# Two transpose banks, ACT as the queue for the weight and restack loads, and scratch stores issued back to back in an eight-core transformer layer

## The chip, the cores and the metric

The kernel runs on the 8 cores of one Trainium2 chip. Each core takes 4 of the 32 sequences, and the cores exchange nothing. The metric is the device time in microseconds (us) of the slowest core; lower is better. PE is TensorE, DVE is VectorE, ACT is ScalarE, POOL is GpSimd, and SP is SyncE, which only issues DMAs here. SPq in a row is the issue of a DMA by SP.

## The reference

One layer on x of shape (32, 2048, 1024): multi-query attention with 8 heads of 128, then a feed-forward part with 128 small experts (32 experts x 4 sets) whose tokens are picked inside groups of 32.

```
x = layernorm(x + attention(x))
# feed-forward, g = 32 tokens per group, s = 4 sets, e = 32 experts
logits   = einsum('bntd,des->bntes', grouped, Wc) + bc + tie
perm     = (logits == max over the tokens t of the group)
permuted = einsum('bntd,bntes->bnesd', grouped, perm)
inner    = relu(einsum('bnesd,esdf->bnesf', permuted, W1) + b1)
result   = einsum('bnesf,esdf->bnesd', inner, W2) + b2
x = layernorm(x + einsum('bnesd,bntes->bntd', result, perm))
```

## The kernel before

Every engine has one list of instructions, written out in program order: `inc(engine, semaphore, n, ...)` appends an instruction that counts a semaphore up when done, `wait(engine, mark)` appends a wait, and `gset`/`gwait` keep the mark after which a buffer may be used again. An engine does its list strictly in order, so a wait on it holds back all that stands behind.

A core does its 4 sequences (s = 0 to 3) one after the other:

1. Projections and attention, with layer norm 1 at the end (`ln1`, 16 ACT instructions, L243).
2. Logits. For each of 4 blocks of 512 tokens, ACT casts x2 to bf16 (`xtile_bf`, L558, 4 instructions); PE transposes it in 8 steps of 4 transposes into the one PSUM tile `pp_tr` (L567); DVE copies each step to `x2t` (L572); then 8 matmuls make the logits (L580), one more adds the tie term (L583), and DVE adds the bias (L588). `xtile_bf` has one buffer, given back by the last copy.
3. The selection: DVE makes `pmT` (L593, L598), and PE and DVE turn it in 16 steps through `pp_tr` into `pmt` (L605, L608).
4. Gather and first expert product, for each of 4 column quarters q4: ACT casts x2 to `x2b` (L627), PE gathers (L638), DVE and ACT evict to `gq` (L649), and PE multiplies by `w_1` (L669). `w_1` has two buffers.
5. Second expert product, restack, and scatter. `emit_e2(q4)` fills `rpn` by 64 casts, half on DVE and half on ACT (L734), with the quarter's weights `w_2t`. `emit_restack(q4)` moves `rpn` to `rpe` in another layout through the DRAM scratch `rp_scratch`: two halves of 64 partitions, each a 2 MB store (L752, 64 rows of 32 KB) and a 2 MB load (L757, pieces of 512 B). `emit_scatter(q4)` multiplies `rpe` by `pmT` (L770, L777) and adds to x2 on DVE (L784). The order of emission is e2(0), restack(0), e2(1), scatter(0), restack(1), e2(2), scatter(1), restack(2), e2(3), scatter(2), restack(3), scatter(3).
6. Layer norm 2 and the stores of y.

What sets the order around the restack: the casts of e2(q4+1) wait until restack(q4) is over (key `rpn`). A restack waits on SP for the scatter before it (key `rpe`) and for all 64 casts by 64 single waits. All four of its DMAs are in SP's list, with a wait on SP between each store and its load.

In sequence 0 the expert weights come as f32 through POOL (cast on the way) and are stored as bf16 to `cw1` and `cw2` by SP; later sequences load those copies from SP's list, `w_2t` for the next quarter at the end of each `emit_e2` (4 DMAs of 512 KB), and `w_1` for the next quarter at the start of a gather stage.

Of the kernel before, what the change touches and what calls it, by code (L numbers as in the profile page):

```python
# [26 lines left out]
def build_nc(cfg):  # L27
# [36 lines left out]
    def bump(n):  # L64
# [50 lines left out]
          for i in range(2)]  # L115
# [23 lines left out]
    pp_tr = nc.alloc_psum_tensor("pp_tr", [128, 512], BF16).ap()  # L139
    pp_w = nc.alloc_psum_tensor("pp_w", [128, 1024], F32).ap()  # L140
# [3 lines left out]
                "sWA", "sWB", "sWC", "sWD", "sWE", "sWS", "sS1a", "sS1b", "sS2", "sS3"]  # L144
# [125 lines left out]
    for s in range(NSEQ):  # L270
# [87 lines left out]
        for qb in range(NQB):  # L358
# [66 lines left out]
            def emit_epilogue_tensor(h):  # L425
                wait("tensor", epi["nm"])
                gwait("tensor", ("tr",))
# [9 lines left out]
                gset(("tr",), av)  # L437
# [66 lines left out]
        def w1_load(q4):  # L504
# [9 lines left out]
            return inc("sync", w1sems[1][q4 % 2], 16,  # L514
                       lambda e, q=q4: e.dma_start(out=w_1[q % 2], in_=cw1[q]))
        if s == 1:
            wait("sync", st_all_ws)
            wait("sync", st_s2_all)
            wait("sync", st_s1a); wait("sync", st_s1b)
        if s > 0:  # L520
            wait("sync", ln1)
        gw1 = {0: w1_load(0)}
        def w2t_load(q4, part):
# [16 lines left out]
            inc("sync", sem, 16, lambda e, q4=q4, c0=c0: e.dma_start(  # L540
                out=w_2t[0][:, c0: c0 + 2048], in_=cw2[q4][:, c0: c0 + 2048]))
            return inc("sync", sem, 16, lambda e, q4=q4, c0=c0: e.dma_start(
# [10 lines left out]
        for tb in range(NQB):  # L553
            cm = None
            gwait("scalar", ("xtbf",))
# [5 lines left out]
            wait("tensor", cm)  # L561
            gwait("tensor", ("x2t",))
            for c in range(CH):
                gwait("tensor", ("tr",))
                tvv = None
                for t4 in range(4):
                    tvv = inc("tensor", "sPE", 1, lambda e, c=c, t4=t4: e.transpose(  # L567
                        pp_tr[:, t4 * 128: t4 * 128 + 128],
                        xtile_bf[:, t4 * 1024 + c * 128: t4 * 1024 + c * 128 + 128],
                        c_ident))  # L570
                wait("vector", tvv)
                cv = inc("vector", "sDVE", 1, lambda e, c=c: e.tensor_copy(  # L572
                    x2t_stage[:, c * 512: c * 512 + 512], pp_tr[:, :]))
                gset(("tr",), cv)
            gset(("xtbf",), cv)
            wait("tensor", cv)
            gwait("tensor", ("pw", 0))
            lgv = None
            for c in range(CH):
                lgv = inc("tensor", "sPE", 1, lambda e, c=c: e.matmul(  # L580
# [22 lines left out]
        for tt in range(NT):  # L603
            gwait("tensor", ("tr",))
            tv2 = inc("tensor", "sPE", 1, lambda e, tt=tt: e.transpose(  # L605
                pp_tr[:, 0:128], pmT[:, tt * 128: tt * 128 + 128], c_ident))
# [339 lines left out]
```

How the kernel before makes its waits and increments, by code:

```python
    def inc(eng, sem, n, buildfn):  # L155
        cnt[sem] += n; v = cnt[sem]
        emit(eng, lambda e, b=buildfn, s=sem, n=n: b(e).then_inc(sems[s], n))
        return (sem, v)
# [1 line left out]
    def wait(eng, mark):  # L160
        if mark is None: return
        sem, v = mark
        emit(eng, lambda e, s=sem, v=v: e.wait_ge(sems[s], v))
```

## Time and profile before

| | before |
|---|---|
| median of 3 runs | 5153.95 us (5148.46 to 5167.36) |
| profiled execution, device time | 5157.47 us |
| its span on the slowest core (core 7) | 5155.9 us |
| spans of the 8 cores | 5117.7 to 5155.9 us |
| mean granted PE clock, by core | 0.654 to 0.663 of full speed |
| busy share PE / DVE / ACT / POOL | 51% / 29% / 35% / 0% |
| DMA traffic of the core | 324.85 MB, mean 63 GB/s |

No engine is busy for more than about half of the span. The chain of work that ended last tells better than the shares what the time consists of, and the timeline of one stage tells what each step there waits for.

### The profile page before, as it was taken

The numbers are of one execution on the slowest core, as the hardware profiler recorded it, in microseconds if no ns is written. First come the engines' busy times: TensorE is split into PE (matmuls) and PEld (weight loads), VectorE is DVE, ScalarE is ACT, GpSimd is POOL, SyncE is SP. The second block draws the span as 40 slices with busy tenths as digits, with TensorE's granted clock in tenths as the row PEclk, the third lists the DMA queues.
The fourth block names the chain that finished last, engine by engine and source line by source line (L and its number), as shares of the span: only waits on it lengthen the run. The fifth ranks groups of instructions, "written<-read, shape, count | busy, mean of one in ns | idle before, by whom it ended". The sixth has DMA issues, their size and how long they took to land.

```text
span 5155.9 us, 64669 instructions; the slowest of 8 cores (5117.7 to 5155.9 us)
## 1 busy us (share of the span) xinstructions
PE 2644.5 (51%) x19792; PEld 1414.7 (27%) x19792; DVE 1489.5 (29%) x3689; ACT 1824.3 (35%) x3808; POOL 18.2 (0%) x35
## 2 busy tenths in 40 slices
PE   4666636332566663543256665453317666546240
PEld 2333314211233331421123332242103333224110
DVE  2322135222232213432322211443223221144232
ACT  0455533210335563330134556232121455523113
POOL 0000000000000000000000000000000000000000
PEclk9687856555667885655576887555557688756555
DMA  4200042475310001036520000105651000100644
GB/s 84 58 17 17 9 98 67 99 152 114 98 41 17 17 6 53 34 82 148 113 95 17 17 17 16 43 34 118 127 122 70 17 17 17 55 20 18 147 98 130
DMA packets 174811, 324.85 MB, mean 63 GB/s; under 512 B 5654, under 2 KB 136982, under 8 KB 168986
## 3 DMA queue, kind: packets, MB, share of 16 engines
q1 hardware_dynamic: 166554, 281.39, 21.3%
q0 software_dynamic: 7936, 39.33, 4.4%
q8 instruction: 184, 3.01, 0.2%
q14 instruction: 137, 1.12, 0.1%
HBM read 239.95 MB, written 120.07 MB: 70 GB/s over the span
## 4 chain that ended last, share of the span: by engine, by line
PE 43%; ACT 18%; DMA 16%; issue 11%; DVE 10%; SPq 1%; ACTq 0%; DVEq 0%; POOL 0%; POOLq 0%
DMA rp_scratch<-rpn 10%; PE pp_pv L397 8%; ACT pT L373 7%; PE pp_s L365 6%; PE pp_w L474 5%; PE pp_s L302 5%; DMA rpe<-rp_scratch 4%; PE pp_s L669 4%; PE pp_s L638 2%; PE pp_s L721 2%; ACT x2b L627 2%; ACT pTn L419 2%; DVE pT L381 2%; PE pp_pv L721 2%; DVE x L482 2%
## 5 line engine op out<-in xcount | busy, mean ns | idle before, releaser
L373 ACT ACTIVATE pT<-pp_s,c_negC 128x512 bf16<-128x512 f32 x1280 | 842.1, 690 | 354.4 <-PE pp_pv L397 207.5
L397 PE MATMUL pp_pv<-vS,pT 128*128 128x129 bf16 x5120 | 620.8, 258 | 395.0 <-DVE pT L381 230.6
L397 PEld LDWEIGHTS pp_pv<-vS,pT 128*128 128x128 bf16 x5120 | 393.7, 112 | 793.3 <-issue 790.1
L365 PE MATMUL pp_s<-qT,kT 128*128 128x512 bf16 x1280 | 600.7, 488 | 0.1
L381 DVE TENSOR_TENSOR pT<-pT,c_zl 128x512 bf16<-128x512 bf16 x512 | 217.7, 425 | 954.8 <-ACT pT L373 954.8
L721 PE MATMUL pp_s<-w_2t,inr 32*64 32x256 bf16 x1024 | 142.5, 402 | 666.0 <-DVE rpn L734 620.3
L302 PE MATMUL pp_s<-xT,w_q 128*128 128x512 bf16 x1024 | 250.5, 413 | 281.3 <-DMA w_kv<-cwkv 212.6
L734 ACT CAST rpn<-pp_s 128x256 bf16<-128x256 f32 x256 | 95.4, 373 | 794.2 <-DMA rpe<-rp_scratch 721.2
L474 PE MATMUL pp_w<-w_o,atT 128*128 128x512 bf16 x1024 | 275.1, 430 | 94.0 <-DVE x L482 79.9
L734 DVE CAST rpn<-pp_s 128x256 bf16<-128x256 f32 x256 | 108.7, 425 | 680.5 <-DMA rpe<-rp_scratch 628.0
L721 PEld LDWEIGHTS pp_s<-w_2t,inr 32*64 32x64 bf16 x1024 | 72.0, 122 | 731.7 <-issue 729.2
L638 PE MATMUL pp_s<-pmt,x2b 32*128 32x128 bf16 x1024 | 128.2, 280 | 267.5 <-ACT x2b L627 252.2
L649 ACT CAST gq<-pp_s 128x256 bf16<-128x256 f32 x256 | 95.3, 372 | 448.0 <-PE pp_pv L638 404.8
L669 PE MATMUL pp_s<-gq,w 128*32 128x64 bf16 x4096 | 226.7, 411 | 17.7 <-ACT gq L649 7.3
L419 ACT ACTIVATE pTn<-pp_pv,rs 128x128 bf16<-128x128 f32 x512 | 146.5, 368 | 244.9 <-DVE rs L412 242.7
L302 PEld LDWEIGHTS pp_s<-xT,w_q 128*128 128x128 bf16 x1024 | 106.6, 104 | 423.9 <-issue 358.0
L669 PEld LDWEIGHTS pp_s<-gq,w 128*32 128x32 bf16 x4096 | 208.9, 142 | 33.0 <-issue 29.4
L770 PE MATMUL pp_w<-c_b,pmT 128*128 128x256 bf16 x256 | 95.4, 373 | 212.4 <-DMA rpe<-rp_scratch 199.7
L784 DVE TENSOR_TENSOR x<-x,pp_w 128x256 f32<-128x256 f32 x256 | 107.9, 421 | 280.4 <-PE pp_w L777 279.8
L649 DVE CAST gq<-pp_s 128x256 bf16<-128x256 f32 x256 | 108.7, 424 | 259.8 <-PE pp_s L638 257.0
L474 PEld LDWEIGHTS pp_w<-w_o,atT 128*128 128x128 bf16 x1024 | 105.8, 107 | 259.5 <-issue 186.1
L307 DVE SCALAR_TENSOR_TENSOR qT<-pp_s,c_bq,c_pe 128x512 bf16<-128x512 f32 x128 | 96.2, 751 | 270.5 <-PE pp_s L302 270.5
(86 smaller groups left out, 2875.5 us busy)
## 6 DMA issues: line engine op xcount, KB each, us to landing
rp_scratch<-rpn SPq DMA_DIRECT2D x32, 2048.0 KB, 15.5
rpe<-rp_scratch SPq DMA_DIRECT2D x32, 2048.0 KB, 14.4
xtile<-x SPq DMA_DIRECT2D x64, 512.0 KB, 3.9
y<-x SPq DMA_DIRECT2D x64, 512.0 KB, 5.0
w<-cw SPq DMA_DIRECT2D x12, 2048.0 KB, 8.0
w_2t<-cw SPq DMA_DIRECT2D x48, 512.0 KB, 7.0
xT<-xT POOLq DMA_DIRECT2D x4, 4096.0 KB, 25.7
w<-w POOLq DMA_DIRECT2D x4, 2048.0 KB, 15.1
```

Source lines behind the costliest of these rows:

```text
L302: mmq = inc("tensor", "sPE", 1, lambda e, ps=ps, c=c, hc=hc, tb=tb: e.matmul(ps[:, :], w_q[:, c * 1024 + hc * 128: c * 1024 + hc * 128 + 128],
L365: return inc("tensor", "sPE", 1, lambda e, kc=kc, ping=ping, h=h, qb=qb: e.matmul(pp_s[ping][:, :], kT[:, kc * 128: kc * 128 + 128], qT[:, ...
L373: ev = inc("scalar", "sACT", 1, lambda e, ping=ping: e.activation(out=pT[ping][:, :], in_=pp_s[ping][:, :], func=AF.Exp, bias=c_negC, scal ...
L381: mv = inc("vector", "sDVE", 1, lambda e, ping=ping, j=j: e.tensor_tensor(pT[ping][:, :], pT[ping][:, :], c_zl[:, (3 - j) * 128: (3 - j) * ...
L397: ping=ping, sub=sub, kc=kc, kcmax=kcmax: e.matmul(bank[:, colo: colo + 129], pT[ping][:, sub * 128: sub * 128 + 128], vS[:, kc * 132: kc ...
L419: e.activation(out=pTn[:, sub * 128: sub * 128 + 128], in_=bank[:, colo: colo + 128], func=AF.Identity, scale=rs[:, sub: sub + 1]))
L474: wv = inc("tensor", "sPE", 1, lambda e, h=h, half=half, t4=t4: e.matmul(pp_w[:, half * 512: half * 512 + 512], atT[:, h * 512 + t4 * 128: ...
L638: gvv = inc("tensor", "sPE", 1, lambda e, j=j, cc=cc, tt=tt, bidx=bidx: e.matmul(banks4g[bidx][:, cc * 128: cc * 128 + 128], x2b[tt % 2][j ...
L649: m = inc(eng2, sem2, 1, lambda e, g=g, bidx=bidx, cp2=cp2: cp2(e)(bass.AP(gq.tensor, gq.offset + g * 128, [[gq.ap[0][0], 128], [NG * 128, ...
L669: cc=cc, q4=q4: e.matmul(ps[b * 32: b * 32 + 32, qq * 64: qq * 64 + 64], w_1[q4 % 2][:, cc * 4096 + es * 32: cc * 4096 + es * 32 + 32], ba ...
L721: q4=q4: e.matmul(ps[half * 64: half * 64 + 64, 0:256], inr[b * 32: b * 32 + 32, q * 64: q * 64 + 64], w_2t[0][b * 32: b * 32 + 32, q * 25 ...
L734: m = inc(eng2, sem2, 1, lambda e, r=r, ps=ps, cp3=cp3: cp3(e)(rpn[:, r * 256: r * 256 + 256], ps[:, 0:256]))
```

## The change

1. A second PSUM tile `pp_tr2` is allocated, and the key `tr` becomes two keys. The 8 transposing steps of the logits stage and the 16 steps of `pmt` alternate between the two tiles. Each logits matmul waits for the copy of its own step in place of the last one.
2. For s > 0 the loads of `w_1` and `w_2t` are issued by ACT in place of SP, with the waits that belong to them.
3. In the restack both stores are issued by SP, one behind the other, each with a semaphore of its own. ACT waits for the scatter before (`rpe`), then for each store, and issues the load of that half. SP no longer waits for `rpe`, nor between the DMAs.

The casts of the logits stage are put into a function, `emit_cast_full`, in unchanged order.

```
+    pp_tr2 = nc.alloc_psum_tensor("pp_tr2", [128, 512], BF16).ap()
...
-            return inc("sync", w1sems[1][q4 % 2], 16,
+            return inc("scalar", w1sems[1][q4 % 2], 16,
                        lambda e, q=q4: e.dma_start(out=w_1[q % 2], in_=cw1[q]))
         if s == 1:
-            wait("sync", st_all_ws)
-            wait("sync", st_s2_all)
-            wait("sync", st_s1a); wait("sync", st_s1b)
-        if s > 0:
-            wait("sync", ln1)
+            wait("scalar", st_all_ws)
+            wait("scalar", st_s2_all)
+            wait("scalar", st_s1a); wait("scalar", st_s1b)
...
-            inc("sync", sem, 16, lambda e, q4=q4, c0=c0: e.dma_start(
+            inc("scalar", sem, 16, lambda e, q4=q4, c0=c0: e.dma_start(
                 out=w_2t[0][:, c0: c0 + 2048], in_=cw2[q4][:, c0: c0 + 2048]))
-            return inc("sync", sem, 16, lambda e, q4=q4, c0=c0: e.dma_start(
+            return inc("scalar", sem, 16, lambda e, q4=q4, c0=c0: e.dma_start(
...
+        trb = [pp_tr, pp_tr2]
...
             for c in range(CH):
-                gwait("tensor", ("tr",))
+                bnk = trb[c % 2]
+                gwait("tensor", ("tr", c % 2))
...
-            gset(("xtbf",), cv)
-            wait("tensor", cv)
+            gset(("xtbf",), cvs[CH - 1])
             gwait("tensor", ("pw", 0))
             for c in range(CH):
+                wait("tensor", cvs[c])
                 lgv = inc("tensor", "sPE", 1, lambda e, c=c: e.matmul(
...
         for tt in range(NT):
-            gwait("tensor", ("tr",))
+            bnk = trb[tt % 2]
+            gwait("tensor", ("tr", tt % 2))
...
                 if q4 >= 1:
-                    wait("gpsimd" if s == 0 else "sync", now("sPE"))
+                    wait("gpsimd" if s == 0 else "scalar", now("sPE"))
                 gw1[q4 + 1] = w1_load(q4 + 1)
...
-                eng_w = "gpsimd" if s == 0 else "sync"
+                eng_w = "gpsimd" if s == 0 else "scalar"
                 wait(eng_w, now("sPE"))
...
         def emit_restack(q4):
-            gwait("sync", ("rpe",))
+            gwait("scalar", ("rpe",))
             for mm_ in rsq_all[q4]:
                 wait("sync", mm_)
             for hh in range(2):
-                sth = inc("sync", "sRS", 16, lambda e, hh=hh: e.dma_start(
+                sth = inc("sync", ["sRSa", "sRSb"][hh], 16, lambda e, hh=hh: e.dma_start(
                     out=bass.AP(drp.tensor, drp.offset + 64 * hh * 16384,
                                 [[16384, 64], [1, 16384]]),
                     in_=rpn[64 * hh: 64 * hh + 64, :]))
-                wait("sync", sth)
-                inc("sync", "sRS", 16, lambda e, hh=hh: e.dma_start(
+                wait("scalar", sth)
+                inc("scalar", "sRS", 16, lambda e, hh=hh: e.dma_start(
```

## Rows read from the trace of the kernel before

**Rows 1.** The page, part 4: the chain that ended last, shares by line.
```profile
DMA rp_scratch<-rpn 10%; PE pp_pv L397 8%; ACT pT L373 7%; PE pp_s L365 6%; PE pp_w L474 5%; PE pp_s L302 5%; DMA rpe<-rp_scratch 4%; PE pp_s L669 4%; PE pp_s L638 2%; PE pp_s L721 2%; ACT x2b L627 2%; ACT pTn L419 2%; DVE pT L381 2%; PE pp_pv L721 2%; DVE x L482 2%
```
**Rows 2.** The page, part 5: the casts to rpn on ACT.
```profile
L734 ACT CAST rpn<-pp_s 128x256 bf16<-128x256 f32 x256 | 95.4, 373 | 794.2 <-DMA rpe<-rp_scratch 721.2
```
**Rows 3.** Timeline of SP, sequence 1, quarters 0 and 1: start us, us, instruction.
```profile
2250.28 0.32 SPq L540 DMA_DIRECT2D w_2t<-cw  x1
...
2251.79 0.81 SPq L542 DMA_DIRECT2D w_2t<-cw  x1
2255.91 0.47 SPq L752 DMA_DIRECT2D rp_scratch<-rpn  x1
2268.13 0.62 SPq L757 DMA_DIRECT2D rpe<-rp_scratch  x1
2268.79 8.01 SPq L752 DMA_DIRECT2D rp_scratch<-rpn  x1
2288.26 0.61 SPq L757 DMA_DIRECT2D rpe<-rp_scratch  x1
...
2336.11 0.47 SPq L752 DMA_DIRECT2D rp_scratch<-rpn  x1
2348.04 0.61 SPq L757 DMA_DIRECT2D rpe<-rp_scratch  x1
```
**Rows 4.** Timeline of the engines there; in brackets the idle time before.
```profile
2250.34 0.37 ACT L734 CAST rpn<-pp_pv 128x256 bf16<-128x256 f32 x1
...
2302.58 0.37 ACT L734 CAST rpn<-pp_s 128x256 bf16<-128x256 f32 x1 [51.87 <-DMA rpe<-rp_scratch]
...
2320.88 0.37 ACT L734 CAST rpn<-pp_pv 128x256 bf16<-128x256 f32 x1 [0.21 <-PE pp_pv L721]
...
2331.96 0.40 PE L777 MATMUL pp_w<-rpe,pmT 128*32 128x256 bf16 x4
```
**Rows 5.** Windows in the first restack; the last column is GB/s moved.
```profile
2258.00:2260.00 2.00, 0.70 (x8) 0.40 (x7) 0.00 (x0) 0.00 (x0) 0.00 (x0) 0.50 1.26 412
2276.00:2278.00 2.00, 0.00 (x0) 0.00 (x0) 0.00 (x0) 0.00 (x0) 0.00 (x0) 0.50 1.19 176
2282.00:2284.00 2.00, 0.00 (x0) 0.00 (x0) 0.00 (x0) 0.00 (x0) 0.00 (x0) 0.50 1.25 475
```
**Rows 6.** Timeline of SP, sequence 0, quarter 0.
```profile
970.05 0.43 SPq L535 DMA_DIRECT2D cw<-w_2t  x1
974.14 0.52 SPq L752 DMA_DIRECT2D rp_scratch<-rpn  x1
```
**Rows 7.** Timeline of the logits stage, sequence 1, first block.
```profile
1970.34 0.58 PE L567 MATMUL pp_tr<-c_ident,xtile_bf 128*128 128x128 bf16 x4 [29.41 <-ACT xtile_bf L558]
...
1971.60 0.59 PE L567 MATMUL pp_tr<-c_ident,xtile_bf 128*128 128x128 bf16 x4 [0.68 <-DVE x2t L572]
...
1980.39 3.89 ACT L558 ACTIVATE xtile_bf<-x 128x1024 bf16<-128x1024 f32 x4 [10.40 <-DVE x2t L572]
...
1980.55 3.57 PE L580 MATMUL pp_w<-x2t,w_c 128*128 128x512 bf16 x8 [0.78 <-DVE x2t L572]
...
1984.91 0.58 PE L567 MATMUL pp_tr<-c_ident,xtile_bf 128*128 128x128 bf16 x4 [0.26 <-PE pp_w L583]
```
**Rows 8.** Timeline of the pmt steps, sequence 1.
```profile
2043.75 0.27 PE L605 MATMUL pp_tr<-c_ident,pmT 128*128 128x128 bf16 x1 [16.80 <-DVE pmT L598]
...
2044.49 0.27 PE L605 MATMUL pp_tr<-c_ident,pmT 128*128 128x128 bf16 x1 [0.48 <-DVE pmt L608]
```
**Rows 9.** Timeline of SP: the first and last of five weight loads behind ln1.
```profile
1966.03 0.33 SPq L515 DMA_DIRECT2D w<-cw  x1
...
1968.37 0.54 SPq L542 DMA_DIRECT2D w_2t<-cw  x1
```
**Rows 10.** Timeline where the gather of quarter 1 begins, sequence 1.
```profile
2097.25 0.28 PE L638 MATMUL pp_s<-pmt,x2b 32*128 32x128 bf16 x2
2097.54 0.32 SPq L515 DMA_DIRECT2D w<-cw  x1
```

More of the change, by code:

```diff
@@ L143, in build_nc @@
                 "sXT0", "sXT1", "sW10", "sW11", "sW20", "sW21",
-                "sWA", "sWB", "sWC", "sWD", "sWE", "sWS", "sS1a", "sS1b", "sS2", "sS3"]
+                "sWA", "sWB", "sWC", "sWD", "sWE", "sWS", "sS1a", "sS1b", "sS2", "sS3", "sRSa", "sRSb"]
     sems, cms = {}, []
@@ L426, in emit_epilogue_tensor @@
                 wait("tensor", epi["nm"])
-                gwait("tensor", ("tr",))
+                gwait("tensor", ("tr", 0))
                 tv = None
@@ L436, in emit_epilogue_tensor @@
                     atT[:, h * 512: h * 512 + 512], pp_tr[:, :]))
-                gset(("tr",), av)
+                gset(("tr", 0), av)
                 epi["av"] = av
@@ L552, in build_nc, with emit_cast_full @@
             wait("scalar", st_wkv)
-        for tb in range(NQB):
+        trb = [pp_tr, pp_tr2]
+        cast_m = {}
+        def emit_cast_full(tb):
+            gwait("scalar", ("xtbf",))
             cm = None
-            gwait("scalar", ("xtbf",))
             for t4 in range(4):
@@ L560, in build_nc @@
                     in_=x2[:, tt * 1024: tt * 1024 + 1024], func=AF.Copy))
-            wait("tensor", cm)
+            cast_m[tb] = cm
+        for tb in range(NQB):
+            emit_cast_full(tb)
+            wait("tensor", cast_m[tb])
             gwait("tensor", ("x2t",))
+            cvs = {}
             for c in range(CH):
-                gwait("tensor", ("tr",))
+                bnk = trb[c % 2]
+                gwait("tensor", ("tr", c % 2))
                 tvv = None
                 for t4 in range(4):
-                    tvv = inc("tensor", "sPE", 1, lambda e, c=c, t4=t4: e.transpose(
-                        pp_tr[:, t4 * 128: t4 * 128 + 128],
+                    tvv = inc("tensor", "sPE", 1, lambda e, c=c, t4=t4, bnk=bnk: e.transpose(
+                        bnk[:, t4 * 128: t4 * 128 + 128],
                         xtile_bf[:, t4 * 1024 + c * 128: t4 * 1024 + c * 128 + 128],
@@ L571, in build_nc @@
                 wait("vector", tvv)
-                cv = inc("vector", "sDVE", 1, lambda e, c=c: e.tensor_copy(
-                    x2t_stage[:, c * 512: c * 512 + 512], pp_tr[:, :]))
-                gset(("tr",), cv)
-            gset(("xtbf",), cv)
-            wait("tensor", cv)
+                cv = inc("vector", "sDVE", 1, lambda e, c=c, bnk=bnk: e.tensor_copy(
+                    x2t_stage[:, c * 512: c * 512 + 512], bnk[:, :]))
+                gset(("tr", c % 2), cv)
+                cvs[c] = cv
+            gset(("xtbf",), cvs[CH - 1])
             gwait("tensor", ("pw", 0))
@@ L603, in build_nc @@
         for tt in range(NT):
-            gwait("tensor", ("tr",))
-            tv2 = inc("tensor", "sPE", 1, lambda e, tt=tt: e.transpose(
-                pp_tr[:, 0:128], pmT[:, tt * 128: tt * 128 + 128], c_ident))
+            bnk = trb[tt % 2]
+            gwait("tensor", ("tr", tt % 2))
+            tv2 = inc("tensor", "sPE", 1, lambda e, tt=tt, bnk=bnk: e.transpose(
+                bnk[:, 0:128], pmT[:, tt * 128: tt * 128 + 128], c_ident))
             wait("vector", tv2)
-            pmv = inc("vector", "sDVE", 1, lambda e, tt=tt: e.tensor_copy(
-                pmt[:, tt * 128: tt * 128 + 128], pp_tr[:, 0:128]))
-            gset(("tr",), pmv)
+            pmv = inc("vector", "sDVE", 1, lambda e, tt=tt, bnk=bnk: e.tensor_copy(
+                pmt[:, tt * 128: tt * 128 + 128], bnk[:, 0:128]))
+            gset(("tr", tt % 2), pmv)
         e1p_marks = {}
```

## The prediction

> **What bounds the kernel now.** I read the chain that ended last first, since no engine is busy for much more than half of the span. Its largest entry by line is no engine: the store `rp_scratch<-rpn` has 10% and the load `rpe<-rp_scratch` 4% [rows 1], some 720 us of 5156. The costliest groups say the same from the other side: the ACT casts to `rpn` are 95 us busy, with 721 us of idle time ended by the restack's load [rows 2]. So the restack, 16 times in the program, stops every engine, and the timeline of one of them is what to read closely.
>
> In it the reader is to see five stretches. The last cast of quarter 0 ends at 2250.34 + 0.37 = 2250.71 [rows 4], and the first store is issued at 2255.91 [rows 3]. SP is done with the last `w_2t` issue at 2252.60; the 3.31 us up to the store are its 64 waits, all long met, at 52 ns each. Store 0 then takes 12.2 us until its load is issued. Store 1, issued right behind, holds SP for 8.01 us and lands 11.46 us after that, and load 1 takes 14.3 us until the casts resume at 2302.58 [rows 3, 4]. From last cast to next cast that is 51.9 us, 46.7 of them from the first store.
>
> In the next quarter the last cast ends at 2321.25, but the store starts only at 2336.11, 14.9 us later [rows 3, 4]. In between PE does the scatter of the quarter before, up to 2332.36, and behind it come the 64 waits, 3.75 us. The store needs neither: only the load overwrites `rpe`. With the 46.5 us of the restack itself that makes 61.4 us from cast to cast.
>
> **Restack, quarters 1 to 3 of sequences 1 to 3 and quarter 3 of sequence 0 (10 times).** SP's 64 waits are now passed one by one as the casts end, and store 0 goes out some 0.1 us behind the last. The scatter, 11.1 us, now lies beside store 0, 11.9 us when nothing else runs (2336.11 to 2348.04) [rows 3, 4]; so the load's wait for `rpe` costs nothing, and if that cover were gone it would cost the difference at most. Store 1 is in the same ring behind store 0 and I let it take a full further 11.5 us: T + 23.5, with T the last cast's end. Load 0 is issued at T + 12.1 and lands 14.3 us later, at T + 26.4. Load 1 is issued at T + 23.5 behind load 0 and follows it at the pace of such loads, 176 GB/s [rows 5], 11.9 us for 2 MB: T + 38.3. With a little for ACT's hand-over I take T + 39.5 against 61.4, and 21.5 us of gain, 10 times: 215 us.
>
> This rests on load 0 and store 1 running beside each other without loss. The rows show it: while load 0 was in flight (it would land alone at 2268.13 + 14.3 = 2282.4), store 1 took 11.46 us from the end of its issue, where an undisturbed one takes 11.93 - 0.47 = 11.46 [rows 3]; and where they met, 475 GB/s were moved against 176 by the load alone [rows 5]. The bounds: if the two stores ran beside each other fully and the two loads too, the end would be T + 12 + 14.4 = T + 26.5; if nothing overlapped at all, T + 11.9 + 11.5 + 14.3 + 14.3 = T + 52. Neither is near the rows: transfers of one direction are not shown beside each other, a load beside a store is.
>
> A rule of the Trainium skill speaks against this sum: "DMA: Bandwidth & Descriptors", section Rules for kernel authors, says that two transfers to disjoint partition halves serialize since both use the same 16 engines, and that spreading DMAs over SP, ACT and GpSimd gives no bandwidth. Rows 5 don't agree for a load met by a store, but the rule makes a rival, below.
>
> **Quarter 0 of sequences 1 to 3 (3 times).** No scatter stands in the way. `w_2t`'s four loads now leave ACT while store 0 leaves SP. In the old order they also met, at 412 GB/s [rows 5], and store 0 took 12.2 in place of 11.9 us [rows 3]. I take T + 40 against T + 51.9: 12 us each, 36 us.
>
> **Quarters 0 to 2 of sequence 0 (3 times).** SP still stores `cw2` and passes its 64 waits before store 0 (970.05 + 0.43 to 974.14) [rows 6], because POOL's loads land late; that part stays. From the store on, 39 us stand against 46.7: 7.7 us each, 23 us.
>
> What is queued behind ACT's new waits? Behind the wait for a store stand only the casts of the next quarter, which wait for the same restack anyway, or layer norm 2, which needs the last scatter. The `w_2t` issues stand where ACT has only that to do. They cost nothing; without this cover they would cost their 2 to 3 us of issue per quarter.
>
> **Two banks in the logits stage (16 blocks).** One step is 1971.60 - 1970.34 = 1.26 us, transposes and then the copy, neither beside the other [rows 7]. With two banks a bank still takes 1.26 us per round but two rounds run, so a step takes 0.63 us; PE's 0.58 us of transposes fit in that. The eighth step starts at 3 x 1.26 + 0.63 = 4.4 us, the matmuls at about 4.9 us where they started at 10.2 (1970.34 to 1980.55), and the last copy ends at 5.6. Then the cast of the next block, 3.89 us, comes to bound: next block at 5.6 + 3.9 + 0.2 = 9.7 us in place of 14.57 (to 1984.91), 4.9 us less. The last block has no cast behind it and gives 5.3. That is 3 x 4.9 + 5.3 = 20 us a sequence, 80 us in all. The ends: nothing, if PE's sequencing took what the bank gives; some 6 us per block, if the cast were hidden too, which one `xtile_bf` excludes.
>
> **Two banks for pmt (64 steps).** A step is 2044.49 - 2043.75 = 0.74 us [rows 8]; halved, that gives 16 x 0.37 = 5.9 us a sequence. The first and the last step are not helped, so 23 us in all.
>
> **What ACT pays.** Behind ln1 five issues stand before the first cast to `xtile_bf`; on SP they lasted from 1966.03 to 1968.91, 2.9 us [rows 9]. No ACT issue is in the trace; SP's are the nearest rows, from 0.32 to 8.01 us [rows 3, 10]. At their pace this is 3 x 2.9 = 9 us; the lower end is 0, if they pass while the last ACTIVATE runs. At the start of quarters 1 and 2 ACT must now wait for PE to finish the product before, and issue one load (0.32 us), before its first `x2b` cast; until now those casts were ready and PE went on at 2097.25 without a wait [rows 10]. That is 6 times between 0.1 and 1.2 us; I take 3 us. The first of these loads (quarter 0) has no wait and stands where ACT is idle. The four waits in sequence 1 are long met. Relieved SP has nothing urgent otherwise: its x and y transfers keep their places.
>
> **Sum.** 5157.5 (the profiled execution's own time) - 215 - 36 - 23 - 80 - 23 + 12 = 4792 us. That execution lay 3.5 us above the median, so 4789; I say 4790.
>
> **Rivals.**
> - *Work is conserved* (0.15): DMAs from two queues only share the engines. Then load 0 beside store 1 gains nothing over one behind the other, and all four make T + 12 (store 0) + 10.5 (store 1's 11.46 less about 1 of start) + 2 x 11.9 (2 MB at 176 GB/s) + 2 for landing = T + 48, 9 us later, 16 times: 4790 + 144 = 4934. For it: the busy share is above 1 in the windows shown. Against it: their GB/s. This is the time by the rule of the Trainium skill above.
> - *ACT's load is held by SP's store* (0.12): one issue can hold another up, as store 1's did for 8.01 us behind load 0. If load 0 is started only when most of store 1 has been taken up, at about T + 17, each restack ends 5 us later: 4790 + 80 = 4870.
> - *ACT becomes the bound and the kernel gets slower* (0.02): if a DMA issue on ACT lasts long, the 15 issues behind ln1 and the 6 at the gathers are on the path. To eat 367 us they would need 17 us each, against 8.01 in the longest row of SP. At 20 us each: 4790 - 12 + 420 = 5198.
> - *The banks give nothing* (0.04): PE, not the bank, sets the step. Then 4790 + 103 = 4893. Against it: the idle 0.68 us in each step [rows 7].
>
> **How the numbers follow.** My forecast has 0.67. Around it lie the granted clock, which every PE stage follows, and the hand-overs: 4730 to 4850 in that case. The range must take in the second and fourth rival whole and the first just: 4720 to 4940. About 0.5% (26 us) is what a measurement of this kernel can tell from no change. Faster 0.97, same 0.01, slower 0.02: only the third rival, or several of the sizes failing together, leads there.
>
> **What would show it.** In the profile after: `rp_scratch<-rpn` issued within 0.5 us of the last cast, beside the scatter; ACT's idle time before L734 from 794 us to about 520; 39 to 40 us from last cast to next cast in quarters 1 to 3; logits blocks 9.7 us apart, the cast and no longer PE ending the wait; pmt steps 0.37 us apart; five issues by ACT before L558. The prediction is wrong in size if load 0 lands much later than 14.3 us after its issue, or store 1 later than 24 us after the last cast; wrong in sign only if ACT's issues last above ten microseconds.

## The result and the profile after

| | before | after |
|---|---|---|
| median | 5150.62 us (5142.35 to 5171.85, 8 runs) | 4902.89 us (4897.72 to 4910.04, 8 runs) |
| ratio after / before | | 0.9515, 95% interval 0.9498 to 0.9532 |
| profiled execution | 5157.47 us | 4910.04 us |
| spans of the 8 cores | 5117.7 to 5155.9 us | 4872.1 to 4908.5 us |
| mean granted PE clock, by core | 0.654 to 0.663 | 0.668 to 0.671 |

The kernel became 4.9% faster. The forecast was 4790 us with a range from 4720 to 4940: the sign is right, the range holds the time, and of the 364 us forecast 248 came. The band that the forecast gave its own case, 4730 to 4850 us, does not hold the time; what holds it is the room that was left for the rivals.

First the page of the kernel after, part 4, the chain that ended last, by engine and by line; it answers to [rows 1].

```profile
PE 40%; ACT 19%; DMA 18%; issue 10%; DVE 10%; ACTq 1%; SPq 0%; DVEq 0%; POOL 0%; POOLq 0%
PE pp_pv L398 8%; DMA rpe<-rp_scratch 8%; DMA rp_scratch<-rpn 7%; ACT pT L374 7%; PE pp_s L366 6%; PE pp_w L475 5%; PE pp_s L303 5%; PE pp_s L677 4%; PE pp_s L646 3%; PE pp_s L729 2%; ACT x2b L635 2%; ACT pTn L420 2%; PE pp_pv L729 2%; DVE pT L382 2%; DVE x L483 2%
```

The store's share fell from 10% to 7%, and the load's rose from 4% to 8%. In us the restack's DMAs have not become shorter on the chain: some 720 us before, 15% of 4908 or some 740 now. Their weight has moved from the stores to the loads, and what went lay in front of them. Parts 3, 5 and 6 of the same page say so too. SP's queue, also called its ring, is q1 and ACT's is q10 (packets, MB, share of the time of 16 engines); then come the ACT casts, which answer to [rows 2], and the DMA issues with their median time from issue to landing.

```profile
q10 hardware_dynamic: 140224, 117.45, 11.8%
q1 hardware_dynamic: 26330, 163.94, 11.3%
...
L742 ACT CAST rpn<-pp_s 128x256 bf16<-128x256 f32 x256 | 95.2, 372 | 714.9 <-DMA rpe<-rp_scratch 647.7
...
rp_scratch<-rpn SPq DMA_DIRECT2D x32, 2048.0 KB, 17.6
rpe<-rp_scratch ACTq DMA_DIRECT2D x32, 2048.0 KB, 24.0
...
w_2t<-cw ACTq DMA_DIRECT2D x48, 512.0 KB, 12.6
```

The idle time of ACT before its casts went from 794 to 715 us, where 520 were forecast. A load needs 24.0 us where it needed 14.4, and a `w_2t` load 12.6 where it needed 7.0.

Next the timeline of ACT and SP in sequence 1, quarter 1 of core 2. It answers to [rows 3, 4].

```profile
2234.88 0.37 ACT L742 CAST rpn<-pp_pv 128x256 bf16<-128x256 f32 x1 [0.20 <-PE pp_pv L729]
2234.95 0.33 ACTq L539 DMA_DIRECT2D w_2t<-cw  x1
...
2235.33 1.09 SPq L760 DMA_DIRECT2D rp_scratch<-rpn  x2
...
2247.83 20.69 ACTq L765 DMA_DIRECT2D rpe<-rp_scratch  x2
2285.69 0.37 ACT L742 CAST rpn<-pp_s 128x256 bf16<-128x256 f32 x1 [50.45 <-DMA rpe<-rp_scratch]
```

The last cast ends at T = 2234.88 + 0.37 = 2235.25, and both stores are issued 0.08 us later. The casts resume at 2285.69, which is T + 50.4. The two DMA steps of the chain in this stretch (start, us) show where the time lies:

```profile
2235.83 22.20 DMA rp_scratch<-rpn
2258.07 0.04 issue
2258.10 27.51 DMA rpe<-rp_scratch
```

The stores end at T + 22.8, the forecast's T + 23.5. Load 0 was issued at T + 12.6, but the end of the pair comes 27.5 us after the last store. That is about what two loads need one behind the other (26.2 us in experiment 3, quarter 3, where nothing else is in flight), with the rest of `w_2t` ahead of them. The DMA queues in the 8 us from load 0's issue (2247.8 to 2255.8; packets, MB, share) show why.

```profile
q1 hardware_dynamic: 51, 1.61, 88.3%
q10 hardware_dynamic: 58, 0.23, 7.3%
```

Store 1 moved 1.61 MB. On ACT's queue only 0.23 MB went, in packets of about 4 KB, while the load's pieces are 512 B: those are `w_2t`, which stands ahead of load 0 there. In quarter 3 no `w_2t` is about, and the 8 us from load 0's issue (2385.4 to 2393.4) have only the store in them:

```profile
q1 hardware_dynamic: 48, 1.57, 94.2%
rpe<-rp_scratch ACTq DMA_DIRECT2D x1, 2048.0 KB, 21.7
```

Load 0 moved next to nothing while store 1 ran: it landed 21.7 us after its issue. The pair of loads ends there 22.5 us after the last store, so some 4 us were gained by the early issue of load 0.

The two bank edits, in sequence 1 of the same core: two of the four casts of the logits stage, the first PE rows of a block, and the `pmt` steps. They answer to [rows 7, 8].

```profile
1904.66 3.89 ACT L559 ACTIVATE xtile_bf<-x 128x1024 bf16<-128x1024 f32 x4
...
1908.91 1.01 PE L573 MATMUL pp_tr<-c_ident,xtile_bf 128*128 128x128 bf16 x8 [29.42 <-ACT xtile_bf L559]
1910.18 1.01 PE L573 MATMUL pp_tr<-c_ident,xtile_bf 128*128 128x128 bf16 x8 [0.25 <-DVE x2t L578]
...
1914.34 3.90 ACT L559 ACTIVATE xtile_bf<-x 128x1024 bf16<-128x1024 f32 x4 [5.78 <-DVE x2t L578]
...
1918.59 0.61 PE L573 MATMUL pp_tr<-c_ident,xtile_bf 128*128 128x128 bf16 x8 [1.61 <-ACT xtile_bf L559]
...
1961.34 0.39 PE L613 MATMUL pp_tr<-c_ident,pmT 128*128 128x128 bf16 x2 [16.80 <-DVE pmT L605]
1962.09 0.39 PE L613 MATMUL pp_tr<-c_ident,pmT 128*128 128x128 bf16 x2 [0.35 <-DVE pmt L616]
```

One PE row now holds two steps, and the next row comes 1.27 us later, so a step takes 0.63 us. The blocks lie 1914.34 - 1904.66 = 9.7 us apart, and PE's wait at the next block is ended by the cast. Two `pmt` steps take 0.75 us.

Last, ACT at the end of layer norm 1, which answers to [rows 9] (the first and last of five issues are shown).

```profile
1886.31 5.77 ACT L244 ACTIVATE x<-x,st_b,st_r 128x1024 f32<-128x1024 f32 x5 [1.07 <-DVE st_b L235]
1891.20 0.36 ACTq L516 DMA_DIRECT2D w<-cw  x1
...
1893.41 0.55 ACTq L541 DMA_DIRECT2D w_2t<-cw  x1
1894.24 10.28 ACT L244 ACTIVATE x<-x,st_b,st_r 128x1024 f32<-128x1024 f32 x9
```

The five issues stand behind all 16 ACTIVATEs in ACT's list. The first went out at 1891.20, while the fifth ACTIVATE ran (until 1892.08) and eleven were still to come. So an issue without a wait of its own does not stay behind the ACTIVATEs before it. The stretch is no longer for it: 1886.31 to 1904.52, 18.21 us, as before the change.

### The profile page after: what moved, and what is told of

The parts are those of the page before. It is cut to its first block, busy times and chain, and to the rows that moved or that the text cites. A ratio compares the mean times of both kernels' runs of the same rounds, so it can differ in the third digit from the quotient of the medians.

```text
span 4908.5 us, 64777 instructions; the slowest of 8 cores (4872.1 to 4908.5 us)
## 1 busy us (share of the span) xinstructions
PE 2599.7 (53%) x19792; PEld 1417.7 (29%) x19792; DVE 1501.1 (31%) x3689; ACT 1835.1 (37%) x3808; POOL 18.2 (0%) x35
## 3 DMA queue, kind: packets, MB, share of 16 engines
q10 hardware_dynamic: 140224, 117.45, 11.8%
q1 hardware_dynamic: 26330, 163.94, 11.3%
## 4 chain that ended last, share of the span: by engine, by line
PE 40%; ACT 19%; DMA 18%; issue 10%; DVE 10%; ACTq 1%; SPq 0%; DVEq 0%; POOL 0%; POOLq 0%
PE pp_pv L398 8%; DMA rpe<-rp_scratch 8%; DMA rp_scratch<-rpn 7%; ACT pT L374 7%; PE pp_s L366 6%; PE pp_w L475 5%; PE pp_s L303 5%; PE pp_s L677 4%; PE pp_s L646 3%; PE pp_s L729 2%; ACT x2b L635 2%; ACT pTn L420 2%; PE pp_pv L729 2%; DVE pT L382 2%; DVE x L483 2%
## 5 line engine op out<-in xcount | busy, mean ns | idle before, releaser
L635 ACT ACTIVATE x2b<-x 128x256 bf16<-128x256 f32 x256 | 109.0, 426 | 196.3 <-DVE pmT L605 98.9
## 6 DMA issues: line engine op xcount, KB each, us to landing
rp_scratch<-rpn SPq DMA_DIRECT2D x32, 2048.0 KB, 17.6
w_2t<-cw ACTq DMA_DIRECT2D x48, 512.0 KB, 12.6
```

Of the source, the lines that this page charges most:

```text
L635: cm2 = inc("scalar", "sACT", 1, lambda e, tt=tt, q4=q4: e.activation(out=x2b[tt % 2], in_=x2[:, tt * 1024 + q4 * 256: tt * 1024 + q4 * 25 ...
```

## The experiments

Eleven kernels ran, in three rounds, each against the kernel before on the same chip. Its medians there were 5147.43 us (experiments 1 to 4), 5141.74 us (5 to 8) and 5146.17 us (9 to 11). T is always the end of the last cast of a quarter. "Quarter 3" is the restack with no `w_2t` beside it. A kernel is set beside the kernel after by these ratios. The theories are about why load 0 gets nothing beside store 1. From the first round on: the two rings take turns by the packet, 32 KB of the store against 512 B of the load (theory 1), or the bytes share the engines and the order plays no part (theory 2, work conserved). From the second: the store only has the earlier place in time (theory 3); `w_2t` costs its time by slowing store 0 (theory 4). From the third: whoever came first is served (theory 5), or ACT's ring loses to SP's whichever is first (theory 6).

**1. banks_only.** The kernel before with the two banks and nothing else.

```
+    pp_tr2 = nc.alloc_psum_tensor("pp_tr2", [128, 512], BF16).ap()
...
+                bnk = trb[c % 2]
+                gwait("tensor", ("tr", c % 2))
```

> The kernel before with the two transpose banks alone (logits stage and pmt); restack, w_1 and w_2t loads stay in SP's list as before. No theory on the restack bears on it. The trace of the changed kernel shows 20.0 us less per sequence in the logits stage and 6 us in pmt: 4 x 26 = 104 us, so 5047 us, a ratio of 0.980 to before. If the banks gave something back elsewhere (the granted clock, a later wait), it would be nearer to 0.985.

Measured: 5044.24 us, ratio 0.9779 (0.9741 to 0.9818), 103 us less between the medians; the interval of the ratio is 94 to 133 us. The forecast's bank terms, 80 + 23, lie in it. What is left for the rest of the change is 248 - 103 = 145 us, with the same uncertainty; 262 were forecast (215 + 36 + 23 - 12).

**2. loads_on_sp.** The kernel after, with the two restack loads back in SP's list in the old order. The stores still leave early, since the wait for `rpe` stands only before load 0.

```
-            gwait("scalar", ("rpe",))
+            grpe = guards.pop(("rpe",), None)
...
-                wait("scalar", sth)
-                inc("scalar", "sRS", 16,
+                wait("sync", sth)
+                if hh == 0:
+                    wait("sync", grpe)
+                inc("sync", "sRS", 16,
```

> The changed kernel, but both restack loads go back to SP's list in the old order (store 0, load 0, store 1, load 1), while the stores still start before the scatter is over. Theory 1, turns of packets: a DMA engine takes SP's and ACT's rings in turn, one packet each, and a store row of 32 KB is one turn; so whatever stands in ACT's ring starves until the stores are over. In one ring load 0 stands ahead of store 1 and lands 14.4 us after its issue, as before; cast to cast 47 us against 48.8 to 50.4 with w_2t and 44.3 without: 4903 - 6 x 3.7 - 3 x 1.8 + 4 x 2.4 + 3 x 1.4 = about 4889 us. Theory 2, work conserved: the order plays no part, load 0 takes its 22 us and more beside store 1, cast to cast stays 49 to 50 us, 4903 us.

Measured: 4915.50 us, ratio 0.9557 (0.9495 to 0.9619), the same as the kernel after within the interval. Its page has the loads at the old 14.4 us:

```profile
rpe<-rp_scratch SPq DMA_DIRECT2D x32, 2048.0 KB, 14.4
```

The timeline of SP in quarter 3 shows what such a load costs the store beside it:

```profile
2392.26 0.61 SPq L767 DMA_DIRECT2D rpe<-rp_scratch  x1
2392.92 7.86 SPq L760 DMA_DIRECT2D rp_scratch<-rpn  x1
2412.21 0.61 SPq L767 DMA_DIRECT2D rpe<-rp_scratch  x1
```

Load 0 and store 1 together take 2412.21 - 2392.26 = 20.0 us, and from cast to cast quarter 3 takes 46.2 to 48.3 us over the four sequences, where the kernel after takes 44.7 to 46.1. Theory 1's 47 us came there; the quarters with `w_2t` took 47.9 to 52.3.

So the two arrangements come out alike: in one ring, load 0 runs first and store 1 follows; in two rings, both stores go first and the loads follow. Stores back to back and loads by ACT, part 3 of the change without the early start, were worth nothing that can be measured. The early start (no wait for the scatter, no 64 waits in a row, and in quarter 0 no `w_2t` issues ahead of the store, which part 2 takes to ACT) and the bank edits carry the whole gain. What each piece of the early start gives by itself was not run.

**3. one_store.** The kernel after with one store of 128 partitions (4 MB) in place of two, and both loads behind it.

```
-            for hh in range(2):
-                sth = inc("sync", ["sRSa", "sRSb"][hh], 16, lambda e, hh=hh: e.dma_start(
...
-                    in_=rpn[64 * hh: 64 * hh + 64, :]))
+            sth = inc("sync", "sRSa", 16, lambda e: e.dma_start(
+                out=bass.AP(drp.tensor, drp.offset, [[16384, 128], [1, 16384]]),
+                in_=rpn[:, :]))
```

> The changed kernel with one store of all 128 partitions (4 MB) in place of two of 64; both loads are issued by ACT when it has landed. Both theories: if a store of 64 partitions is held by the half of the SBUF ports it reaches, 4 MB leave in 11 to 13 us in place of 22, and the loads follow in 24 us: 37 to 38 us from cast to cast where there is no w_2t load, and some 43 where there is. 4903 - 4 x 7 - 12 x 7 = about 4790 us. If the ports do not bind, the store takes 22 us and the kernel is slower than the changed one, since load 0 then starts 10 us later: 4903 + some 20 us or more.

Measured: 4818.25 us, ratio 0.9343 (0.9306 to 0.938), 1.8% below the kernel after. The timelines of ACT and SP in quarter 3 have one wait for a store of 4 MB; the end is at 2388.91, T + 37.6 (T = 2350.99 + 0.37 = 2351.36).

```profile
2350.99 0.37 ACT L742 CAST rpn<-pp_pv 128x256 bf16<-128x256 f32 x1 [0.20 <-PE pp_pv L729]
2351.45 0.32 SPq L759 DMA_DIRECT2D rp_scratch<-rpn  x1
2362.71 8.26 ACTq L764 DMA_DIRECT2D rpe<-rp_scratch  x2
```

The 4 MB left the SBUF in 2362.71 - 2351.45 = 11.3 us, where the two halves take 22.3 in the same quarter of the kernel after (2372.93 to 2395.23). With `w_2t` beside it the store takes longer; the median of all is 15.6 us. The Trainium skill, "DMA: Bandwidth & Descriptors", section Rules for kernel authors, says that transfers to disjoint partition halves serialize, so one 128-partition transfer should be used. The trace agrees with the advice. That the halves share the engines is not the whole of it, though, since then one transfer of 4 MB would take as long as the two: here a store of 64 partitions takes as long for 2 MB (11.9 us, [rows 3]) as one of 128 for 4 MB.

**4. store_4k.** Theory 1 tried by smaller store pieces: a row of 32 KB written as 8 pieces of 4 KB.

```
-                                [[16384, 64], [1, 16384]]),
+                                [[16384, 64], [2048, 8], [1, 2048]]),
```

> The changed kernel with each store row of 32 KB described as 8 pieces of 4 KB; bytes, queues and order are the same. Theory 1, turns of packets: ACT's ring gets its turn eight times as often. w_2t lands in 8 to 10 us in place of 12 to 22, load 0 lands within 18 us of its issue though store 1 runs beside it, cast to cast 40 to 44 us in place of 49 to 50: 4903 - 16 x 7 = about 4790 us. Theory 2, work conserved: cutting the rows changes nothing or costs a little, 49 to 51 us, 4900 to 4920 us.

Measured: 4911.53 us, ratio 0.9533 (0.9478 to 0.9588). This tests nothing, and the page of its profile says why: q1 has the same number of packets as after. Pieces that touch were joined again.

```profile
q1 hardware_dynamic: 26330, 163.94, 11.3%
```

**5. store_512.** The same idea, with gaps, so that nothing can be joined: pieces of 512 B, 1 KB apart, in a scratch twice as large.

```
-                                [[16384, 64], [1, 16384]]),
+                                [[32768, 64], [512, 64], [1, 256]]),
```

> The changed kernel with each 32 KB store row written as 64 pieces of 512 B that lie 1 KB apart in the scratch (the run store_4k named pieces that touch, and its packet count, 26330 on SP's queue, shows that they were joined again). Theory 1, turns of packets: now ACT's ring gets a turn for every 512 B or few KB of the store. The w_2t loads land within 9 us in place of 12 to 22 after their issue, and in the 8 us from load 0's issue on, beside store 1, ACT's queue moves at least a third of the bytes, where it moves an eighth now. Theory 2, work conserved and shared by bytes whatever the packets: the split stays near one to seven. The total is no test: a stream of 512 B pieces runs at 176 GB/s, a store of 32 KB rows at 201, so I expect the restack no shorter than T + 48, and the kernel at 4900 to 5000 us.

Measured: 4917.82 us, ratio 0.955 (0.948 to 0.962). Now q1 has 155354 packets, and `w_2t` lands in 7.9 us beside the stores instead of 12.6. For `w_2t` it came as theory 1 said (within 9 us). For load 0 it did not (a third of the bytes was asked for); the window is the 8 us from its issue in quarter 3, where no `w_2t` is about.

```profile
q1 hardware_dynamic: 2803, 1.44, 88.9%
q10 hardware_dynamic: 456, 0.23, 9.6%
```

With packets of the same size on both queues, the store still moved 1.44 MB and the load 0.23 MB. Over the whole run a load lands after 20.2 us (median) in place of 24.0, but a store after 22.7 in place of 17.6, and the sum is the same.

**6. two_rings.** Store 1 is issued only when store 0 has landed, the moment at which ACT issues load 0. So the two start together, in two rings.

```
+                if hh == 0:
+                    wait("sync", sth)
                 wait("scalar", sth)
```

> The changed kernel, but SP issues store 1 only when store 0 has landed, so that load 0 (ACT's ring) and store 1 (SP's ring) start in the same moment, as in the kernel before but in two rings. Theory 1, turns of packets: load 0 is starved by store 1 and lands 20 us or more after its issue, store 1 lands 12 to 13 us after its issue, and the loads end at T + 12.5 + 12 + 22 to 25 = T + 47 to 50; about 4910 us. Theory 3, the order in time alone decides (load 0 must not stand behind store 1's descriptors, as in the kernel before): the pair takes 19 to 20 us as before, cast to cast 46 us without w_2t, 4880 us or less.

Measured: 4933.77 us, ratio 0.9584 (0.9523 to 0.9645). The window is the 8 us from the issue of both, quarter 3.

```profile
q1 hardware_dynamic: 48, 1.57, 95.3%
q10 hardware_dynamic: 1, 0.00, 0.0%
rpe<-rp_scratch ACTq DMA_DIRECT2D x1, 2048.0 KB, 24.1
rp_scratch<-rpn SPq DMA_DIRECT2D x1, 2048.0 KB, 12.3
```

Store 1 landed 12.3 us after its issue, as if alone, and load 0 24.1 us after its own. Theory 3 falls as it was stated: the store takes everything without having been issued earlier. Both issues start at 2404.30; the store's is done after 0.45 us and the load's after 0.58, so who was first by a tenth of a microsecond is not settled.

**7. w2t_behind.** The four `w_2t` loads are issued behind load 0.

```
+                if hh == 0 and q4 in w2_pending:
+                    wait("scalar", w2_pending[q4])
+                    gw2[q4 + 1] = w2t_load(q4 + 1, 0)
+                    gw2b[q4 + 1] = w2t_load(q4 + 1, 1)
```

> The changed kernel with the four w_2t loads of sequences 1 to 3 issued by ACT behind load 0 in place of ahead of it. With the stores starving ACT's ring, w_2t stands ahead of load 0 in that ring and costs its 5 to 6 us of transfer after the stores: quarters with w_2t take 49 to 50 us from cast to cast, the one without 44. Theory 1: moving it behind load 0 but ahead of load 1 saves nothing of the sum (it is still in the ring before load 1): 48 to 50 us, 4900 us; w_2t's landing moves later, by 15 us or more, and PE waits for it without a cost. Theory 4, w_2t's share is not its bytes but that it slows store 0 (24.35 us for both stores with it, 21.75 without): then 2 us a quarter come back, 9 x 2 = 18 us, 4885 us.

Measured: 4921.11 us, ratio 0.9558 (0.9516 to 0.9599), no gain; in the quarters with `w_2t` 51.5 to 53.6 us from cast to cast. The 18 us of theory 4 did not come. But the timeline of ACT in quarter 0 shows a price that no theory named: the issue behind load 0's is held for 15.8 us, and load 1 stands behind it.

```profile
2186.79 0.61 ACTq L768 DMA_DIRECT2D rpe<-rp_scratch  x1
2187.48 15.81 ACTq L539 DMA_DIRECT2D w_2t<-cw  x1
...
2205.22 0.59 ACTq L768 DMA_DIRECT2D rpe<-rp_scratch  x1
```

Load 1 goes out at 2205.22, T + 30.6 (T = 2174.65), where it goes out at T + 25.0 in the same quarter of the kernel after. So this run changes two things, the place of the `w_2t` bytes and the time of load 1, and does not decide about theory 4.

**8. one_load.** The scratch is laid out so that one load of 128 partitions, behind both stores, fetches all 4 MB.

```
-                                [[16384, 64], [1, 16384]]),
+                                [[32768, 64], [1, 16384]]),
...
+            inc("scalar", "sRS", 16, lambda e: e.dma_start(
+                out=rpe[:, :].rearrange("p (g d) -> p g d", d=256),
+                in_=bass.AP(drp.tensor, drp.offset,
+                            [[256, 128], [32768, NG], [1, 256]])))
```

> The changed kernel with one load of all 128 partitions (4 MB in pieces of 512 B, the scratch laid out for it) in place of two of 64, issued when both stores have landed. If the load's pace is set by its 512 B pieces, 176 GB/s, it takes 25 us from T + 22.3: cast to cast 47 us without w_2t, 49 to 52 with it, 4910 us. If it is set by the half of the ports that 64 partitions reach, it takes 13 to 16 us: cast to cast 36 to 39, with w_2t about 41, 4903 - 12 x 9 - 4 x 7 = about 4770 us.

Measured: 4795.47 us, ratio 0.9341 (0.9268 to 0.9414). It gives up all overlap of a load with a store and is 1.8% faster than the kernel after. Quarter 3, ACT and PE:

```profile
2354.11 0.69 ACTq L765 DMA_DIRECT2D rpe<-rp_scratch  x1
...
2371.37 0.37 PE L778 MATMUL pp_w<-c_b,pmT 128*128 128x256 bf16 x1 [27.94 <-DMA rpe<-rp_scratch]
```

4 MB in 2371.37 - 2354.11 = 17.3 us. The two loads of experiment 3, in the same quarter and with nothing beside them either, need 2388.91 - 2362.71 = 26.2 us, and the kernel after needs 22.5 from the last store's landing, a part of load 0 having come before. Its q10 has 41664 packets in place of 140224 for the same bytes, so this run changes two things at once, the number of partitions and the size of the packets. Which of them gives the pace isn't told apart.

**9. load_first.** Store 1 is held until ACT has issued load 0: a tiny ACTIVATE of 128x1 behind the issue, for which SP waits.

```
+                if hh == 1:
+                    wait("sync", inc("scalar", "sACT", 1, lambda e: e.activation(
+                        out=st_b[:, 0:1], in_=c_eps, func=AF.Copy)))
```

> The changed kernel, with SP's store 1 held until ACT has issued load 0 (ACT then does one 128x1 ACTIVATE of its own, and SP waits for that), so load 0 goes out 1 us ahead of store 1, in two rings. The run two_rings showed load 0 starved when both start together, and the run store_512 showed that the size of the store's packets is not what starves it, so theory 1 as it stood has fallen. Theory 5, first come: what counts is whose descriptors reach the DMA engines first; load 0 ahead of store 1 gives the pair 19 to 20 us as in one ring, load 0 lands 14 to 15 us after its issue, cast to cast 46 us without w_2t, 4900 us. Theory 6, two rings: a load in ACT's ring loses to a store in SP's whichever is first; load 0 lands 20 us or more after its issue as in two_rings, cast to cast 48 us, 4930 us.

Measured: 4876.63 us, ratio 0.9473 (0.9456 to 0.949), a little below the kernel after. In quarter 3 load 0 is issued at 2383.14 and store 1 at 2384.05, and the window of 8 us from there has turned round:

```profile
q10 hardware_dynamic: 2064, 1.06, 70.5%
q1 hardware_dynamic: 16, 0.52, 18.8%
rpe<-rp_scratch ACTq DMA_DIRECT2D x1, 2048.0 KB, 20.2
rp_scratch<-rpn SPq DMA_DIRECT2D x1, 2048.0 KB, 13.1
```

A head start of 0.9 us makes 1.06 MB out of 0.00 for the load. Theory 5 holds in its direction. It is not a strict order: load 0 landed after 20.2 us, which is what theory 6 said, not after 14 to 15; in the 6 us that follow the window the store moved 1.57 MB and the load 0.29. The median of the loads is 19.4 us, and quarter 3 ends at T + 43.5. In the quarters with `w_2t`, which stands ahead of load 0, little was gained (46.1 to 51.1 us from cast to cast against 48.8 to 50.4).

**10. chunk_two_loads.** `rpn` is stored in four column pieces of 128 partitions while the casts still run; two loads behind them. The first half of the next `w_2t` is loaded by SP in the middle of the casts, the second by ACT behind the restack's loads.

```
+                if r % 16 == 15:
+                    wait("sync", rsq_marks[-2]); wait("sync", rsq_marks[-1])
+                    k = r // 16
+                    chunk_marks[q4, k] = inc("sync", ["sRSa", "sRSb", "sRSc", "sRSd"][k], 16,
+                        lambda e, k=k: e.dma_start(
+                            out=bass.AP(drp.tensor, drp.offset + k * 4096,
+                                        [[16384, 128], [1, 4096]]),
+                            in_=rpn[:, k * 4096: k * 4096 + 4096]))
```

> The changed kernel with the stores taken off the path: SP stores rpn in four column pieces of 128 partitions, each as soon as its 16 casts are done, so three of the four lie beside the casts; SP loads the first half of the next w_2t when PE is through with it, and ACT the second half behind the restack's loads. Both loads stay as they are. No theory of rings is at stake, since no store is in flight when the loads run: the last piece lands some 5 us after the last cast, the loads start at T + 5 in quarter 0 and at T + 11.2 (the scatter) in the others, and take 25 us: cast to cast 30 and 36 us against 48.8 and 50, without w_2t 36 against 44. 4903 - 3 x 19 - 6 x 14 - 4 x 8 - 3 x 15 = about 4690 us.

Measured: 4716.45 us, ratio 0.9169 (0.9142 to 0.9196). In sequence 1 it takes 34.4 to 38.0 us from cast to cast in the quarters with `w_2t`, where it takes some 50 in the kernel after, and 38.0 in quarter 3. The early pieces take most of the stores' 22 us off the path. What is left are the scatter and the two loads, which land 25.4 us after their issue (median).

**11. chunk_one_load.** The early pieces of 10, here of 64 partitions in the layout of 8, with the one load of 8.

```
+                    for hh in range(2):
+                        chunk_marks[q4, k] = inc("sync", ["sRSa", "sRSb", "sRSc", "sRSd"][k], 16,
+                            lambda e, hh=hh, k=k: e.dma_start(
+                                out=bass.AP(drp.tensor, drp.offset + hh * 16384 + k * 4096,
+                                            [[32768, 64], [1, 4096]]),
+                                in_=rpn[64 * hh: 64 * hh + 64, k * 4096: k * 4096 + 4096]))
```

> The run before with the scratch laid out so that one load of 128 partitions replaces the two of 64; the run one_load had it land in 17.2 us. The pieces are stored as two halves of 64 partitions each. Cast to cast 23 us in quarter 0 and 29 us in the others: some 7.5 us less than the run before, 16 times, 4690 - 120 = about 4570 us. If a stage hidden until now came to bound (the second half of w_2t, which PE needs 9 us after the casts resume), it would show as a wait of PE for w_2t and cost up to 5 us in 9 quarters, 4615 us.

Measured: 4589.57 us, ratio 0.893 (0.8896 to 0.8965), the fastest of all, 6% below the kernel after. The timeline of ACT in sequence 1:

```profile
2154.13 0.71 ACTq L775 DMA_DIRECT2D rpe<-rp_scratch  x1
...
2171.18 0.37 ACT L744 CAST rpn<-pp_s 128x256 bf16<-128x256 f32 x1 [17.09 <-DMA rpe<-rp_scratch]
```

And its chain by engine, which stands against the 18% for DMA of the kernel after:

```profile
PE 45%; ACT 21%; issue 11%; DVE 11%; DMA 10%; ACTq 1%; DVEq 0%; SPq 0%; POOL 0%; POOLq 0%
```

The stores have left the path here: the load is issued 0.5 us after the scatter before has ended (its last matmul row ends at 2153.67), and 17 us later the casts go on. DMA's share of the chain is 10%, where it is 18% in the kernel after.

## Why the prediction was right, and where it was too large

- **Banks, logits stage (80) and pmt (23).** Right. From the first cast of the logits stage to its end, core 2 in sequence 1 takes 60.9 us before (1949.12 to 2009.98) and 40.9 after (1904.66 to 1945.51), the 20 us of the forecast; blocks are 9.7 us apart, the cast ends PE's wait, and banks_only gives 103 us for the sum (94 to 133). That the medians differ by exactly the forecast's sum is luck within that interval. The rival that the banks give nothing is out.
- **What ACT pays (12).** Next to nothing of it is seen. The five issues behind layer norm 1 (9 us forecast) went out within it, and the stretch kept its length: the lower end named for this part, 0, was the true value. At the gathers (3 us) the wait that was forecast is there: at 2058.59 PE begins the gather of quarter 1 after a wait of 1.33 us for the `x2b` cast. But before the change it waited there too, for DVE. Over the whole run PE's idle time before the gathers that an engine ended grew by some 2 us.
- **Stores beside the scatter.** Right in the main: issued 0.1 us behind the last cast, and both done at T + 22.8 in quarter 1 and T + 22.4 in quarter 3 of sequence 1 (T + 23.5 forecast). With `w_2t` beside them they could take longer, T + 25.0 in quarter 0 and T + 24.6 in quarter 1 of sequence 2, past the 24 us that the forecast named as a sign of being wrong in size. The scatter beside them cost nothing visible.
- **The step that failed** is "load 0 and store 1 running beside each other without loss", in the term Restack. It put the end at T + 39.5. Measured on core 2 in sequence 1: T + 44.9 in quarter 3 (2372.84 to the scatter at 2417.71), T + 48.8 in quarter 0 (2167.75 to 2216.58), T + 50.4 in quarter 1. With the forecast's own 61.4 and 51.9 us for before, that makes 4 x 16.5 + 6 x 11.0 + 3 x 3.1 = 141 us, beside the 145 us that banks_only leaves for the rest. In quarters 0 to 2 of sequence 0, where 23 us were forecast, nothing came: 68.1, 66.2 and 65.3 us from cast to cast before, 68.2, 66.0 and 66.3 after. The forecast had 274 in all these places. (Its 21.5 us for 61.4 - 39.5 should be 21.9, which would have made it 4 us more.) Banks and restack together make some 244 of the 248 us, so little is left that would ask for the granted clock, which differs too (0.654 to 0.663 before, 0.668 to 0.671 after). Put in another way: the restack itself, from its first store, took 46.5 to 46.7 us before and takes 44.8 to 50.4 now. What was gained is the 14.9 us (5.2 in quarter 0) by which it begins earlier, and run 2, which has the early start without the two queues, gained as much.
- **Why it failed.** The row behind it [rows 3, 5] shows a load that was first in its ring, with a store behind it. From that row the forecast took that a load and a store share without loss, in any order. The row does not show so much: from load 0's issue at 2268.13 to store 1's landing at 2288.26 the pair takes 20.1 us, where one behind the other would be 14.3 + 11.9 = 26.2. The 8.01 us for which store 1's issue was held were part of the price, and the forecast left them out. It had both done 14.3 us after load 0's issue. The change puts the store first. In run 6 both start at one moment, in run 9 the load is 0.9 us ahead, and its part in 8 us is 0.00 or 1.06 MB. What is shown is thus that a small lead decides who gets the first 8 us; how the DMA engines come to it is open. Packet turns alone don't explain it (run 5), nor does the `w_2t` in front (quarter 3 of the kernel after has none). Even with the lead the pair took 20.2 us, as in one ring, so no run shows the sharing without loss that the sum rests on. The other assignment, loads on SP and stores on ACT, was not run.
- **A second part of the same term.** Quarters with `w_2t` end 4.0 to 5.6 us later than quarter 3. The forecast let `w_2t` pass beside store 0 at no cost, on [rows 5]. In quarter 1 its 2 MB lie ahead of load 0 in ACT's ring, and its packets are still in the window shown. Run 7 moved them behind load 0 and got nothing, but there load 1 also went out later, so whether it is the bytes, the slower stores (24.4 us in quarter 0 against 21.8 in quarter 3) or both is open. Runs 10 and 11 load half of them during the casts.
- **The rivals.** Both that were to end later lay near, and neither is the mechanism as stated. "Work is conserved" (T + 48, 4934 us) gives the size of quarter 0 and too much for quarter 3, and run 9 shows that load and store can overlap. "ACT's load is held by SP's store" (4870 us, T + 44.5) meets quarter 3 by its number and has the right cause, the store, but held load 0 for 5 us, and by its issue: load 0's issue took 0.6 us, and its bytes waited for nearly the whole store. The rule of the Trainium skill that the forecast weighed ("DMA: Bandwidth & Descriptors", section Rules for kernel authors), that halves serialize and more queues bring no bandwidth, came nearer than the forecast's reading of [rows 5]: run 2, with one queue for the whole restack (`w_2t` stays on ACT's), is as fast as the kernel after.
- **Sign.** The rival in which ACT's issues make the kernel slower asked for 17 us each on the path. None on that path came near: the five behind layer norm 1 took 0.36 to 0.83 us, those at the gathers 0.33. The row of 20.69 us above holds two load issues with the wait for store 1 between them; a single load issue took up to 11.1 us (median 3.4), more than the ten microseconds that the forecast named as a sign of a wrong direction, but where ACT has nothing else to do.

## What to carry to other kernels

A row that shows two transfers sharing well holds for the order in which they were issued there; before counting on it, look which of them was first, and bound the other order by the sum of both. In a store and load through DRAM, the number and shape of the transfers was worth more than the queues: one of 128 partitions in place of two of 64 gave 1.8% when done for the stores, 1.8% when done for the loads (whose packets grew with it), and a second queue gave nothing. Most was gained by starting the stores piece by piece while the casts ran (3.6% below the kernel after, 6% with the one load), since a store that is on no path needs no overlap with a load.

## What the hardware showed that was not expected

- A load of 512 B pieces in one ring moved 0.00 MB in the 8 us after its issue when a 2 MB store was issued in another ring at the same moment (1.57 MB moved), and 1.06 MB against 0.52 when it was issued 0.9 us ahead.
- Two stores of 64 partitions took 22.3 us together, one of 128 with the same 4 MB 11.3 us; two loads of 64 with nothing beside them took 26.2 us, one of 128, with larger packets, 17.3 us (all in quarter 3 of sequence 1).
- ACT issued DMAs that stand behind 16 ACTIVATEs of its list while the fifth of them ran, at 1891.20, where the last ended at 1904.52.
- An issue behind a 2 MB load of 512 B pieces, with a store running in the other ring, was held for 15.8 us on ACT.
- Store pieces that touch in DRAM were joined: 26330 packets with rows of 32 KB and with rows cut in 4 KB.
